# Two macaron stages on one core: cosines later in the queue of VectorE, and half of the residual added on GpSimd

## The chip, the cores and the metric

One core of a Trainium2 chip runs the whole program. The metric is the device time of one execution in microseconds (us). The time before is the median of three runs.

## The reference, cut to what matters

The program is a chain of six blocks on `x`, 16 sequences of 256 tokens with 128 channels: a macaron half block, attention with ALiBi, the same half block again, a mixture of experts, linear attention, and the mixture of experts again. The change lies in the first kind, which runs twice:

```python
x = x + 0.5 * _L0_ffn_ref(_layernorm(x), ...)     # twice, attention between them

def _layer(x, wqkv, qs, ksc, wo, lg, lb, w1, b1, w2, b2):
    q, k, v = split(shift_token(x) @ wqkv)        # 8 heads of 64
    q, k = rotary_xpos(l2norm(q) * qs, l2norm(k) * ksc)
    x = x + local_attention(q, k, v) @ wo         # windows of 64, one back
    h = layernorm(shift_token(x)) * lg + lb
    a, g = split(h @ w1 + b1)
    return x + (a * gelu(g)) @ w2 + b2

for l in range(2):                                # DEPTH
    x = _layer(x, wqkv[l], ...)
```

So the running value `y` of a sequence goes through two layers, and then `x = x + 0.5 * y`.

## The kernel before, in words

Engines are named PE (TensorE), DVE (VectorE), ACT (ScalarE), POOL (GpSimd). Each has its own queue, and the order in each queue is written out by hand; semaphores, one per kind of step, hold them together. `X` holds the residual stream of all sequences with channels on partitions, `Y` the running value of the stage, with its upper 64 channels shifted by one token, so that `shift_token` costs nothing. That is why steps on `Y` that have to undo the shift come in two halves of 64 partitions (`halves()`).

A stage `ffn(f)` works through 32 items: 16 sequences in layer 0 (items 0 to 15), then the same in layer 1 (16 to 31). It is software pipelined. In step k, counted from 0, item k is new (projections `qk`, squares, rotation, norm), item k-1 is in the middle (scores, maxima, exponentials, `attend`) and item k-2 is old (output projection, layer norm, up, gelu, `gated`, down, `resid2`). While k is 13 or less, layer norm of sequence k+2 is prepared beside it (`x_center`, `x_square`, `x_rstd`, `normed`). I speak of a step from one start of `k_out` (line 910) to the next, which is once in each k from 1 on.

What each engine does in a step, in its order:

- DVE: `o_norm(i-2, 1)`, `k_out` (L910, L911), `resid` (L975), `cosines` of tile 0 (L924), `s_max` of group 0 (two L948), `y_center` (L981), `s_max` of groups 1 and 2 (L953), `m_split`, `y_normed` (L985), `sums` of tile 0 (L930), `m_out` (L969), `cosines` and `sums` of tile 1, `clip` (L935), `gated` (three L992), `x_center` (L1013), `qk_norm` of tile 0 (L941), `resid2` (L1000 and, in layer 1, L1006), `qk_norm` of tile 1, `o_norm(i-1, 0)` (L916).
- POOL: for each of two tiles `sines` (two L490) and `rotated` (L498, the sum of cosine and sine parts, so it waits for the cosines of the tile), then `split_h` of the next item (L515, L517) and `normed` (two L505).
- ACT: copies of q and k out of PSUM (L594) and their squares (L599), `square` and `rstd` of the layer norm, `copy_v`, `gelu` with a table load ahead and behind it, `x_square` (L649), `rnorm` (L607, L608), which waits for `clip`, then three exponentials (L622), `recips` and `x_rstd`.
- PE: `qk_T` (L1332), `qk(i, 0)` (L1323 to L1325), `proj` (L1464), `scores` (L1339 and L1392), `y_mean`, `qk(i, 1)`, whose second half (g = 1) waits for `s_max` of group 0 because it writes into that PSUM bank, `y_var`, `v_proj`, `m_T`, `up`, `x_mean`, `scores_T`, `down`, `attend(i-1, 0)` (from L1445, waits for two of the exponentials), `x_var`, `attend(i-1, 1)`.

Two chains matter. `clip`, `rnorm`, the exponentials and `attend` follow one another through three engines. And `qk_norm` of a tile waits for both `rnorm` and `rotated`. The second part of `qk_T`, after which the next `k_out` starts, waits for `o_norm(i-1, 0)`.

In layer 1 `resid2` adds the down product and b2 to `Y` (L1000, two halves), waits for it, and adds half of `Y` to `X` (L1006, two halves).

## Time and profile before

| | us |
|---|---|
| median of three runs | 2471.24 (2462.63 to 2471.93) |
| the profiled execution | 2476.3 |
| its span | 2474.5 |

| engine | busy us | share of the span |
|---|---|---|
| PE | 2133.3 | 86% |
| DVE | 1762.1 | 71% |
| ACT | 1464.2 | 59% |
| POOL | 1056.6 | 43% |

The mean granted clock of TensorE is 0.94 of full speed. The two stages `ffn(0)` and `ffn(1)` lie from about 60 to 880 us and from about 1270 to 2084 us of the span.

In the timeline rows below, the first number is the start in us from the span's start, the second the duration in us, then engine, line, operation, what it writes and reads, shapes and count; in brackets stands how long the engine sat idle before it and what it waited for. Neighbours that are alike are merged into one row with their count, and the duration is then that of all. Rows of one engine can overlap by some 0.1 us, since an instruction starts while the one before is still draining.

### The profile page before, as it was taken

The numbers are of one execution on the slowest core, as the hardware profiler recorded it, in microseconds if no ns is written. First come the engines' busy times: TensorE is split into PE (matmuls) and PEld (weight loads), VectorE is DVE, ScalarE is ACT, GpSimd is POOL, SyncE is SP. The second block draws the span as 40 slices with busy tenths as digits, with TensorE's granted clock in tenths as the row PEclk, the third lists the DMA queues.
The fourth block names the chain that finished last, engine by engine and source line by source line (L and its number), as shares of the span: only waits on it lengthen the run. The fifth ranks groups of instructions, "written<-read, shape, count | busy, mean of one in ns | idle before, by whom it ended". The sixth has DMA issues, their size and how long they took to land. (4 is left out here: it accounts for less than half of the span.)

```text
span 2474.5 us, 56322 instructions
## 1 busy us (share of the span) xinstructions
PE 2133.3 (86%) x23398; PEld 1572.0 (64%) x23398; DVE 1762.1 (71%) x2815; ACT 1464.2 (59%) x2389; POOL 1056.6 (43%) x800
## 2 busy tenths in 40 slices
PE   2799999999889868999878999999999897597968
PEld 1477676666666645555536767766666664495758
DVE  3678788788788637777727787887888884563556
ACT  0577676666666525666536776766667674363635
POOL 4656555454545210000036565555545450550245
PEclk8899999999999969999959999999999998698979
DMA  7000000089999990000000000000000003121022
GB/s 150 1 2 2 2 2 2 2 88 119 113 134 133 135 133 6 2 2 2 2 1 1 2 2 2 2 1 2 2 2 2 1 1 74 56 66 37 35 75 79
DMA packets 211376, 90.91 MB, mean 37 GB/s; under 512 B 79700, under 2 KB 206721, under 8 KB 210996
## 3 DMA queue, kind: packets, MB, share of 16 engines
q1 hardware_dynamic: 202596, 72.27, 23.7%
q0 software_dynamic: 6080, 11.76, 1.5%
q10 hardware_dynamic: 2448, 3.28, 0.6%
q8 instruction: 187, 3.06, 0.6%
q14 instruction: 65, 0.53, 0.1%
HBM read 24.31 MB, written 63.41 MB: 35 GB/s over the span
## 5 line engine op out<-in xcount | busy, mean ns | idle before, releaser
L490 POOL TENSOR_TENSOR work<-work,rot_tables 128x512 f32<-128x512 f32 x256 | 411.0, 1626 | 483.8 <-ACT work L594 483.8
L498 POOL TENSOR_TENSOR work<-work 128x1024 f32<-128x1024 f32 x128 | 304.5, 2379 | 53.0 <-DVE work L924 45.7
L1323 PE MATMUL psum<-qkv_w_hi,h_hi 128*128 128x512 f32 x384 | 189.6, 494 | 90.0 <-DVE small L948 87.7
L924 DVE TENSOR_TENSOR work<-work,rot_tables 128x1024 f32<-128x1024 f32 x128 | 211.0, 1648 | 19.2 <-ACT work L594 17.4
L941 DVE TENSOR_TENSOR work<-work,small 128x1024 f32<-128x1024 f32 x128 | 166.9, 1306 | 76.3 <-ACT small L608 72.1
L1081 DVE TENSOR_REDUCE small<-psum 128x4 f32<-128x1024 f32 x128 | 156.6, 1224 | 88.3 <-PE psum L1582 86.6
L1482 PE MATMUL psum<-centered,ffn_w 128*128 128x256 f32 x768 | 192.2, 402 | 3.0 <-DVE centered L985 2.9
L705 ACT ACTIVATE work<-psum 128x1024 f32<-128x1024 f32 x128 | 131.1, 1024 | 92.7 <-PE psum L1582 92.6
L1420 PE MATMUL psum<-work 64*128 64x128 f32 (+1 forms) x2048 | 179.3, 305 | 0.0
L632 ACT ACTIVATE squared<-centered 128x256 f32<-128x256 f32 x64 | 26.8, 419 | 244.9 <-DVE centered L981 244.9
L1482 PEld LDWEIGHTS psum<-centered,ffn_w 128*128 128x128 f32 x768 | 147.7, 199 | 30.7 <-DVE centered L985 4.5
L1453 PE MATMUL psum<-work,v 128*32 128x192 f32 (+1 forms) x4096 | 163.0, 299 | 0.3 <-issue 0.3
L1323 PEld LDWEIGHTS psum<-qkv_w_hi,h_hi 128*128 128x128 f32 x384 | 74.7, 195 | 138.5 <-DVE small L948 114.2
L1325 PE MATMUL psum<-qkv_w_hi,h_lo 128*128 128x512 f32 x384 | 157.0, 409 | 2.1 <-issue 2.1
L1324 PE MATMUL psum<-qkv_w_lo,h_hi 128*128 128x512 f32 x384 | 156.4, 407 | 0.0
L930 DVE TENSOR_REDUCE small<-qk_squares 128x16 f32<-128x1024 f32 x128 | 154.9, 1210 | 1.5 <-ACT qk_squares L599 1.5
L622 ACT ACTIVATE work<-psum 128x768 f32<-128x768 f32 (+1 forms) x192 | 155.1, 873 | 0.9 <-PE psum L1420 0.8
L505 POOL TENSOR_TENSOR y_all<-centered,squared 64x256 f32<-64x256 f32 x64 | 46.8, 731 | 246.1 <-ACT squared L654 243.6
L559 POOL DMA_INDIRECT h_area<-rows,position x64 | 62.9, 983 | 198.9 <-DVE position L1163 172.3
L763 ACT ACTIVATE qk_squares<-psum,work 128x128 f32<-128x128 f32 x312 | 89.3, 369 | 91.8 <-PE psum L1742 91.8
L1420 PEld LDWEIGHTS psum<-work 64*128 64x128 f32 x2048 | 142.9, 188 | 0.0
L594 ACT ACTIVATE work<-psum 128x1024 f32<-128x1024 f32 x128 | 130.5, 1020 | 16.0 <-PE psum L1325 16.0
(279 smaller groups left out, 5401.9 us busy)
## 6 DMA issues: line engine op xcount, KB each, us to landing
h_area<-mean_weights SPq DMA_DIRECT2D x24, 2048.0 KB, 27.7
tile_x<-h_area SPq DMA_DIRECT2D x39, 128.5 KB, 2.1
stage<-in_consts ACTq DMA_DIRECT2D x1, 2817.0 KB, 12.0
tile_x<-h_area SPq DMA_DIRECT2D x39, 64.5 KB, 1.8
work<-in_x SPq DMA_DIRECT2D x4, 512.0 KB, 27.7
expert_w<-in_ew SPq DMA_DIRECT2D x1, 2048.0 KB, 8.6
expert_w<-in_ew SPq DMA_DIRECT2D x8, 256.0 KB, 6.8
work<-y_tokens SPq DMA_DIRECT2D x4, 512.0 KB, 6.2
```

Source lines behind the costliest of these rows:

```text
L490: last = pool.tensor_tensor(b[:, :, :, o_], a[:, :, :, i_], tab[:, l, 1, t, :, o_].unsqueeze(2).to_broadcast([P, 2, HEADS, 32]), ALU.mult)
L498: pool.tensor_tensor(rC[:, t, :], rC[:, t, :], rB[:, t, :], ALU.add).then_inc(f_sum, 1)
L622: act.activation(PT[:, hs, a:a + w].rearrange("p (h b) j -> p b h j", b=2), PS[:, bs, 0:m * w].rearrange("p b (h j) -> p b h j", h=m), ACT ...
L924: dve.tensor_tensor(g(rC[:, t, :]), g(rA[:, t, :]), tab[:, l, 0, t, :, :].unsqueeze(2).to_broadcast([P, 2, HEADS, DH]), ALU.mult)\
L941: dve.tensor_tensor(c_, c_, sm[0][:, 96 + 16 * t:112 + 16 * t].unsqueeze(2).to_broadcast([P, 16, DH]), ALU.mult).then_inc(f_nrm, 1)
L1081: dve.tensor_reduce(dst, PS[:, 0:2, :].rearrange("p b (t j) -> p b t j", t=TILES), AX, ALU.max, negate=True).then_inc(a_smax, 1)
L1323: pe.matmul(out, hi, w_hi, start=True, stop=False)
L1324: pe.matmul(out, hi, w_lo, start=False, stop=False)
L1325: return pe.matmul(out, lo, w_hi, start=False, stop=True)
L1420: last = pe.matmul(PS[:, bs[h % 2], o:o + w], kT[rows_(h), h // 2, j * P:(j + 1) * P], qT[rows_(h), h // 2, i0:i0 + w], start=False, stop= ...
L1453: last = pe.matmul(PS[32 * q:32 * q + 32, (4, 2)[a], z * T + lo:z * T + hi], V[i % 2][:, j, d:d + 32], PT[:, 4 * a + q, src:src + hi - lo] ...
L1482: last = pe.matmul(PS[:, b, o:o + T], fw[:, l, o2 + c * P:o2 + (c + 1) * P], ycen[:, :], start=True, stop=True)
```

## The change

It has four parts.

1. In the queue of DVE, `cosines(i, 0)` moves from ahead of `s_max(i-1, 0)` to behind `y_normed`. Behind it come `m_out`, `sums(i, 0)`, `cosines(i, 1)`, then `gated(i-2)`, which stood behind `clip` and now stands ahead of `sums(i, 1)` and `clip`.
2. In layer 1, POOL makes half of `Y` as it is after `resid` and before the down product (two scalings of 64x256 into `ocen`) and adds it to `X` (one sum of 128x256). It does so in steps k = 18 to 33, between `rotated` of tile 0 and `sines` of tile 1.
3. In layer 1, `resid2` no longer writes `Y`. One DVE instruction of 128x256 adds down product, b2 and `X` into `X`. For this the w2 and b2 of layer 1 are halved once at the start, on DVE.
4. Those who waited for `f_res2` of every item now wait for `f_res2` in layer 0 and for `x_done` in layer 1 (`items_done`).

```diff
+        def items_done(eng, i):
+            f, k = (i - 1) // ITEMS, (i - 1) % ITEMS
+            if i > 0 and k < SEQS:
+                eng.wait_ge(f_res2, f * SEQS + k + 1)
+            elif i > 0:
+                eng.wait_ge(x_done, 2 * SEQS * f + k - SEQS + 1)
...
+                def half_resid(i):
+                    _, s = layer_of(i)
+                    pool.wait_ge(f_res, i + 1)
+                    pool.wait_ge(f_sum, min(2 * (i + 2) + 1, 2 * ITEMS * (f + 1)))
+                    n = 3 * (f * SEQS + s)
+                    for h, (r, c) in enumerate(halves()):
+                        pool.tensor_scalar(ocen[r, :], Y[r, s, c], 0.5, None, ALU.mult).then_inc(f_half, 1)
+                        pool.wait_ge(f_half, n + h + 1)
+                    pool.tensor_tensor(X[:, s, :], X[:, s, :], ocen[:, :], ALU.add).then_inc(f_half, 1)
+                    pool.wait_ge(f_half, n + 3)
+
-                for k in range(-2, ITEMS):
+                for k in range(-2, ITEMS + 2):
                     i = f * ITEMS + k
                     for t in range(TILES):
-                        if k >= 0:
+                        if 0 <= k < ITEMS:
                             sines(i, t)
                             rotated(i, t)
+                        if t == 0 and k - 2 >= SEQS:
+                            half_resid(i - 2)
...
-            last.then_inc(fold, 1)
+            link(last)
+            w2r = rest[DEPTH - 1][:, o3 - o1:o3 - o1 + HC * P]
+            link(dve.tensor_scalar(w2r, w2r, 0.5, None, ALU.mult))
+            dve.tensor_scalar(b2[:, DEPTH - 1:DEPTH], b2[:, DEPTH - 1:DEPTH], 0.5, None, ALU.mult).then_inc(fold, 1)
...
+                    if l < DEPTH - 1:
                         for r, c in halves():
+                            last = dve.scalar_tensor_tensor(out=Y[r, s, c], in0=PS[r, 7, 0:T], scalar=b2[r, l:l + 1],
+                                                            in1=Y[r, s, c], op0=ALU.add, op1=ALU.add)
+                        last.then_inc(f_res2, 1)
+                    else:
+                        dve.wait_ge(f_half, 3 * (f * SEQS + s + 1))
+                        dve.scalar_tensor_tensor(out=X[:, s, :], in0=PS[:, 7, 0:T], scalar=b2[:, l:l + 1],
+                                                 in1=X[:, s, :], op0=ALU.add, op1=ALU.add).then_inc(x_done, 1)
...
-                    if new:
-                        cosines(i, 0)
                     if mid:
                         s_max(i - 1, 0)
...
                     if old:
                         y_normed(i - 2)
                     if new:
-                        sums(i, 0)
+                        cosines(i, 0)
                     if mid:
                         m_out(i - 1)
                     if new:
+                        sums(i, 0)
                         cosines(i, 1)
+                    if old:
+                        gated(i - 2)
+                    if new:
                         sums(i, 1)
                         clip(i)
-                    if old:
-                        gated(i - 2)
```

## Rows read from the trace of the kernel before

**Rows 1.** Waits of PE in the whole run: total, times, longest, in us.

```profile
PE psum L1323 <- DVE small L948: 87.7, 61, 2.0
```

**Rows 2.** Stretches of one step: length, busy PE, PEld, DVE, ACT, POOL, clock, DMA.

```profile
299.63:323.44 23.81, 22.93 (x278) 16.82 (x274) 19.03 (x28) 17.32 (x27) 14.23 (x10) 1.00 0.01 2
394.85:417.58 22.73, 21.79 (x274) 16.20 (x269) 18.40 (x27) 16.24 (x24) 13.73 (x8) 1.00 0.01 2
1631.48:1655.31 23.83, 21.79 (x274) 16.20 (x270) 19.48 (x28) 16.24 (x24) 12.74 (x8) 1.00 0.01 1
741.54:765.61 24.07, 22.02 (x274) 16.28 (x269) 20.23 (x29) 16.23 (x24) 12.73 (x8) 1.00 1.24 125
```

**Rows 3.** DVE in one step with k over 17: start, duration, line.

```profile
745.97 2.33 DVE L924 TENSOR_TENSOR work<-work,rot_tables 128x1024 f32<-128x1024 f32 x1
748.34 1.29 DVE L948 TENSOR_REDUCE small<-psum 128x4 f32<-128x512 f32 x2
...
752.15 0.43 DVE L985 TENSOR_TENSOR centered<-centered,squared 128x256 f32<-128x256 f32 x1
752.50 1.21 DVE L930 TENSOR_REDUCE small<-qk_squares 128x16 f32<-128x1024 f32 x1
...
753.96 1.51 DVE L924 TENSOR_TENSOR work<-work,rot_tables 128x1024 f32<-128x1024 f32 x1
...
756.62 0.18 DVE L935 TENSOR_SCALAR small<-small 128x32 f32<-128x32 f32 x1
756.79 1.27 DVE L992 SCALAR_TENSOR_TENSOR gated<-psum,b,gelu 128x256 f32<-128x256 f32 x3
...
760.95 0.98 DVE L1000 SCALAR_TENSOR_TENSOR y_all<-psum,b,y_all 64x256 f32<-64x256 f32 x2 [0.39 <-PE psum L1493]
761.97 0.85 DVE L1006 SCALAR_TENSOR_TENSOR x_all<-y_all,x_all 64x256 f32<-64x256 f32 x2
762.85 1.23 DVE L941 TENSOR_TENSOR work<-work,small 128x1024 f32<-128x1024 f32 x1
764.11 1.29 DVE L916 TENSOR_TENSOR o_T<-psum,work 128x512 f32<-128x512 f32 x2
```

**Rows 4.** PE in the same step.

```profile
745.65 0.73 PE L1392 MATMUL psum<-kT_bf,qT_bf 64*128 64x128 bf16 x16
...
747.31 0.40 PE L1325 MATMUL psum<-qkv_w_hi,h_lo 128*128 128x512 f32 x1
749.68 0.50 PE L1323 MATMUL psum<-qkv_w_hi,h_hi 128*128 128x512 f32 x1 [1.97 <-DVE small L948]
```

**Rows 5.** POOL in the same step.

```profile
744.72 2.50 POOL L490 TENSOR_TENSOR work<-work,rot_tables 128x512 f32<-128x512 f32 x2 [7.64 <-ACT work L594]
...
753.11 3.48 POOL L490 TENSOR_TENSOR work<-work,rot_tables 128x512 f32<-128x512 f32 x2 [2.31 <-ACT work L594]
756.67 2.36 POOL L498 TENSOR_TENSOR work<-work 128x1024 f32<-128x1024 f32 x1
```

**Rows 6.** POOL and DVE together in another step, at its clip.

```profile
679.70 2.36 POOL L498 TENSOR_TENSOR work<-work 128x1024 f32<-128x1024 f32 x1
...
679.93 2.16 DVE L935 TENSOR_SCALAR small<-small 128x32 f32<-128x32 f32 x1
```

**Rows 7.** ACT in three steps: that from 741.54, from 299.63, from 394.85.

```profile
758.72 0.23 ACT L607 ACTIVATE small<-small 128x32 f32<-128x32 f32 x1
...
315.72 0.42 ACT L649 ACTIVATE squared<-centered 128x256 f32<-128x256 f32 x1
316.04 0.21 ACT L607 ACTIVATE small<-small 128x32 f32<-128x32 f32 x1
...
410.93 0.23 ACT L607 ACTIVATE small<-small 128x32 f32<-128x32 f32 x1
```

**Rows 8.** Two POOL lines over the whole run: ns min/median/max, starts, shapes.

```profile
L515 POOL CAST h_hi<-y_all x64: 387/397/1397, 63.8 to 2011.8; 128x256 fp32r<-128x256 f32 x64
...
L505 POOL TENSOR_TENSOR y_all<-centered,squared x64: 717/732/742, 62.1 to 1608.0; 64x256 f32<-64x256 f32 x64
```

More of the change, by code:

```diff
@@ L295, in build @@
             ("st", "p", "den", "o", "rec", "o_norm", "proj", "resid")]
-        f_mean, f_cen, f_lsq, f_var, f_rstd, f_norm, f_up, f_g, f_u, f_down, f_res2 = [sem(f"ffn_{n}") for n in
-            ("mean", "centered", "squared", "var", "rstd", "normed", "up", "gelu", "gated", "down", "resid2")]
+        f_mean, f_cen, f_lsq, f_var, f_rstd, f_norm, f_up, f_g, f_u, f_down, f_res2, f_half = [sem(f"ffn_{n}") for n in
+            ("mean", "centered", "squared", "var", "rstd", "normed", "up", "gelu", "gated", "down", "resid2", "half_resid")]
         o_mean, o_cen, o_sq, o_var, o_rstd = [sem(f"pre_{n}") for n in
@@ L512, in split_h @@
                     else:
-                        pool.wait_ge(f_res2, i - SEQS + 1)
+                        items_done(pool, i - SEQS + 1)
                     free(pool, f_qk, 3 * (i - 1))
@@ L998, in resid2 @@
                     dve.wait_ge(f_down, i + 1)
-                    for r, c in halves():
-                        last = dve.scalar_tensor_tensor(out=Y[r, s, c], in0=PS[r, 7, 0:T], scalar=b2[r, l:l + 1],
-                                                        in1=Y[r, s, c], op0=ALU.add, op1=ALU.add)
-                    last.then_inc(f_res2, 1)
-                    if l == DEPTH - 1:
-                        dve.wait_ge(f_res2, i + 1)
-                        for r, c in halves():
-                            last = dve.scalar_tensor_tensor(out=X[r, s, :], in0=Y[r, s, c], scalar=0.5, in1=X[r, s, :],
-                                                            op0=ALU.mult, op1=ALU.add)
-                        last.then_inc(x_done, 1)
+                    if l < DEPTH - 1:
+                        for r, c in halves():
+                            last = dve.scalar_tensor_tensor(out=Y[r, s, c], in0=PS[r, 7, 0:T], scalar=b2[r, l:l + 1],
[5 more added lines that the diff above has]
+                                                 in1=X[:, s, :], op0=ALU.add, op1=ALU.add).then_inc(x_done, 1)
                 def x_center(n):
@@ L1460, in proj @@
                     pe.wait_ge(f_on, 2 * i + 2)
-                    free(pe, f_res2, i)
+                    items_done(pe, i)
                     pe.wait_ge(o_rstd, min(f * SEQS + i % ITEMS + 4, SEQS * (f + 1)))
@@ L1503, in x_var @@
                     pe.wait_ge(o_sq, n + 1)
-                    free(pe, f_res2, f * ITEMS + max(n % SEQS - 3, 0))
+                    items_done(pe, f * ITEMS + max(n % SEQS - 3, 0))
                     pe.matmul(PS[:, 7, T:2 * T], ones[:, :], osq[:, :], start=True, stop=True).then_inc(o_var, 1)
```

## The prediction

> **What bounds the kernel now.** I read the waits of TensorE (PE) first. In the two macaron stages `ffn(0)` and `ffn(1)` one wait stands above all others: the second group of `qk(i, 1)` waits for `s_max(i-1, 0)`, 87.7 us in 61 waits [rows 1]. The reader is to see there that the releaser is VectorE (DVE), a pair of reduces of 1.29 us together [rows 3], not long ones. The table by stretch takes four single steps, each from one start of `k_out` to the next [rows 2]: 23.81 us where a sequence is still being prepared beside it (k = 1 to 13), 22.73 (k = 14), 23.83 (k = 15 to 17) and 24.07 (k = 18 to 31). TensorE is busy 22 to 23 of these, at full clock. So these 31 steps, twice, are near TensorE's own time but for this wait.
>
> The DVE rows of one step of the last kind [rows 3] show why. Times below are from its `k_out`, at 741.54. The cosines of tile 0 stand in the queue ahead of `s_max`: they start at 4.43 and end at 6.76, and only then do the two reduces run, to 8.09. TensorE's last matmul before is at 5.77, its next could issue at about 6.02, and it issues at 8.14 [rows 4].
>
> The same rows show a second thing. The cosines take 2.33 there, 1.51 for tile 1, and L941, of the same size, 1.23. The GpSimd (POOL) rows [rows 5] give the reason: two sines ran from 744.72 to 747.22, and the cosines ended 1.08 after that. In tile 1 the cosines end at 755.47, and the second sine, 1.25 by itself, ends 1.12 later, at 756.59. So an instruction of one engine waits until that of the other is through, and goes on about 1.1 after it. The clip `L935`, 0.18 by itself, took 2.16 where the 2.36 us rotation of GpSimd had started 0.23 before it [rows 6]. `gated`, which reads PSUM, keeps its duration beside the same rotation. The Trainium skill, SBUF — State Buffer, section "SBUF: two separate sides", has this as an exclusive lock that the first comer holds for its whole instruction. These rows bear that out.
>
> **The change, part by part.** *Cosines behind `y_normed`.* `s_max` waits for its scores alone: its scores are the first eight of sixteen matmuls that take 0.73 from 4.11 [rows 4], so with the hand-over it starts at about 4.55. It ends at 5.86, and TensorE goes on at 6.02 in place of 8.14: its part of the step moves up 2.12, and `y_normed` with it, from 10.61 to 8.49. From there DVE's queue counts. With the spacings of the rows [rows 3]: cosines 0 at 8.84 to 10.07; `m_out` and `sums` 0 (1.46 from 752.50 to 753.96) from 9.97; cosines 1 ask at 11.43. GpSimd could not add up tile 0 before 10.12, and its 2.36 end at 12.48. Cosines 1 therefore end at 13.58, 1.1 later.
>
> *`gated` ahead of `sums` 1 and `clip`.* Now `clip` starts 1.15 after the end of cosines 1, `sums` 1 between them. `gated`, 1.27 of which 0.08 overlap its neighbour, comes in too: 13.58 + 1.15 + 1.19 = 15.92. ScalarE's `rnorm` waits for `clip`, and its exponentials and TensorE's `attend` wait behind `rnorm`. Before, `clip` was at 15.08 and `rnorm` at 17.18 [rows 7], behind a table load; moved up by 2.12 it could run at 15.06. Now `clip` is last.
>
> Where a sequence is prepared, `x_center` follows `clip` on DVE, and ScalarE squares it before `rnorm`. `clip` 15.92 to 16.10 (the second sine ends at 13.58 + 1.12 + 1.25 = 15.95, so it hardly waits), `x_center`, of the size of `y_normed` (0.43), 16.09 to 16.51, square 16.55, and `rnorm` 0.33 behind the square as now: 16.88. It was at 16.41 [rows 7], and the step ended 7.40 after it. So 24.28 in place of 23.81: **0.47 longer, 13 steps, +6.1.** The 1 us that TensorE gains in the front of such a step is given back.
>
> k = 14: now `rnorm` at 16.08 [rows 7] and 6.65 to the end. New: `rnorm` 16.14, but GpSimd's rotation 1 (16.03 to 18.45, behind `clip`) holds up `qk_norm` 0 to 19.55; the residual (0.95) and `qk_norm` 1, behind the split of h, end at 21.6, `o_norm` at 22.3, and k_out comes 0.81 after `o_norm` as at 764.80 [rows 3]: 23.1, +0.35. The three steps that take 23.83 now come to the same 23.1: -2.2.
>
> *Half the residual on GpSimd, k = 18 to 31.* It goes between rotation 0 and the sines of tile 1: two scalings of 64x256, one add of 128x256, each waited for. No row shows a scaling on GpSimd. The nearest are the cast of 128x256, 0.40, one input, and the product of 64x256, 0.73, two inputs [rows 8]; I take 0.45, near the one with one input, and keep 0.40 to 0.73 (nothing lets it cost less than a cast). The Trainium skill, GPSIMD Engine Reference, section "Elementwise — side-by-side cycle accounting", gives 769 ns for 512 elements at best, so an estimate of 0.38 for 256; by it the sum would be 4 us less. The add: 512 columns take 1.25 and 1024 take 2.36 [rows 5], so 256 take 0.69. A wait between them costs 0.08 (756.59 to 756.67). The first has its 0.13 of start behind it when cosines 1 let go: 0.32 + 0.08 + 0.45 + 0.08 + 0.69 + 0.08 = 1.70. So the sines start at 15.28, the first ends at 16.53, `clip` (asked 15.92) at 16.66, `rnorm` 16.70; sine 2 ends at 17.78, `qk_norm` 0 at 18.88, rotation 1 at 21.12, the cast of `split_h`, next in GpSimd's queue, at 21.52, `qk_norm` 1 at 22.62, `o_norm` at 23.28, and the next `k_out` at 24.09. It is at 24.07 now: **no gain in 14 steps.** In place of TensorE's wait stands GpSimd's queue: cosines late, rotation, half, sines, rotation in a row. Behind these waits in its queue is `split_h(i+1)`, which ends by 23.2, in time for `qk(i+1, 0)`.
>
> *The down product in one sum.* It removes the two 64x256 of L1006 (0.85) [rows 3] and makes one 128x256 of the two of L1000 (0.98): -1.35 of DVE in such a step, beside GpSimd's queue, so worth nothing there. At the stage's end, where nothing is beside it, it is worth 1.35, and the step before some 0.35: -1.7. The new wait for `f_half` (15.2) is 2 us ahead of the down product; behind it in DVE's queue would stand `qk_norm` 1. Halving w2 and b2 at the start is two small DVE instructions, 384 columns at no more than 0.46 (1.23 for 1024) and 0.18, ahead of the first mean: +0.6. The new waits `items_done` count other semaphores of the same events: nothing.
>
> **Sum.** Each stage +6.1 + 0.35 - 2.2 + 0 - 1.7 = +2.5; twice 5, and 0.6: **+5.6** on the 2476.3 of the profiled execution (span 2474.5), so 2481.9. That execution is 5.1 above the median of the runs, 2471.2. On the median: **2477**.
>
> **Rivals.** *The clip falls behind rotation 1.* In the preparation steps `clip` asks at 15.92, and rotation 1 at 15.95 + 0.08 = 16.03: 0.11 between them. If `gated` is that much later, `clip` waits out the 2.36, as in [rows 6]: `rnorm` 19.2, +2.8 in 13 steps, +2.4 for k = 14, +1.3 in three: 41 a stage in place of 2.5, **2554**. For it: the margin. Against it: the margin now is 0.05 (756.62 and 756.67), and the clip takes 0.18 there. It decides in the whole row of steps at once, since they repeat.
>
> *The half sum is dear:* 0.73 a scaling, +0.56 in 28 steps, **2492**.
>
> *GpSimd fits better:* 0.40 a scaling, and `qk_norm` 1 before the cast (-0.40): -0.5 in 28 steps, **2463**.
>
> *No engine holds the other up after all,* in the new order: `clip` near 15.0, TensorE's wait gone and nothing late in its place, so all but some 6 of the 87.7: **2389**. Against it are [rows 3], [rows 5] and [rows 6].
>
> **How the numbers follow.** Forecast 0.50, clip behind the rotation 0.14, dear half 0.13, better fit 0.18, nothing held up 0.05. The forecast alone is 2477 +- 9. The range reaches to the dear half and beyond the better fit, 2445 to 2510, and leaves out the first and the last rival, 0.19 together. A measurement can tell about 0.5%, 12.4 us, from no change. Faster by more: 0.05 + 0.10 of the better fit + 0.05 of the forecast, where I have laid something out too late, = 0.20. Slower by more: 0.14 + 0.11 of the dear half + 0.15 of the forecast's upper part = 0.40. The rest, 0.40, within.
>
> **What would show it.** TensorE's wait for L948 falls from 87.7 to under 10, which all but the clock agree on. In its place TensorE waits, at the first matmul of `attend`, for ScalarE's exponentials, over 1 us a step. Cosines of tile 0 take 1.23, those of tile 1 about 2.2, each. Clip in steps 18 to 31 stretches to some 0.7. Steps come to 24.3, 23.1 and 24.1. It is wrong if the preparation steps are shorter than 23.8 (DVE not late), near 26.6 (the clip waits out the rotation), or if steps 18 to 31 leave 23.5 to 24.7.

## The result, and the profile after

| | kernel before | changed kernel |
|---|---|---|
| median, us (runs) | 2470.86 (4) | 2505.61 (4) |
| lowest to highest, us | 2462.63 to 2471.93 | 2504.51 to 2509.64 |
| profiled execution, us | 2476.3 | 2504.51 |
| its span, us | 2474.5 | 2502.4 |

The changed kernel is slower: the ratio to the kernel before is 1.0139, with a 95% interval of 1.0109 to 1.017. That is inside the range of the prediction (2445 to 2510), but 28.6 above its figure of 2477 and 4 below its upper end; slower by more than 0.5% had a chance of 0.40. One of the ten executions of `order_only` below, 3387.78 us at a mean granted clock of 0.555, is in its median but not in its ratio.

The busy times of the changed kernel (engine, us, share of the span, instructions):

```profile
PE 2132.2 (85%) x23398; PEld 1577.1 (63%) x23398; DVE 1740.5 (70%) x2721; ACT 1463.6 (58%) x2389; POOL 1156.7 (46%) x896
```

TensorE has the same work as before (2133.3), DVE has 22 us less, GpSimd has 100 us more. TensorE's waits have other releasers (total, times, longest, us):

```profile
PE psum L1468 <- ACT work L643: 57.1, 62, 3.9
PE psum L1355 <- DVE o_T L940: 52.6, 29, 1.9
```

The wait for the maxima, 87.7 us in 61 [rows 1], has no row of more than 0.2 us now. In its place stand the wait of `attend` (L1468) for the exponentials and, 29 times, the wait of `qk_T` (L1355) for `o_norm` of up to 1.9 us.

Single steps of the changed kernel, in the columns of [rows 2]; the last two rows are the first 5 us of the two steps above them:

```profile
306.14:330.38 24.24, 22.88 (x278) 16.82 (x272) 20.11 (x29) 17.32 (x27) 14.12 (x10) 1.00 0.01 2
403.10:426.31 23.21, 21.88 (x274) 16.29 (x268) 20.30 (x27) 16.23 (x24) 12.62 (x8) 1.00 0.01 2
597.31:623.87 26.56, 23.48 (x274) 17.44 (x270) 18.82 (x27) 16.34 (x24) 15.78 (x11) 0.94 1.22 125
623.87:648.83 24.96, 21.87 (x274) 16.28 (x269) 18.82 (x27) 16.23 (x24) 15.86 (x11) 1.00 1.19 113
597.31:602.30 4.99, 4.99 (x22) 3.79 (x18) 1.92 (x2) 4.02 (x4) 1.02 (x1) 0.66 1.11 157
623.87:628.80 4.93, 4.93 (x51) 3.55 (x47) 3.13 (x5) 3.91 (x4) 1.75 (x2) 1.00 1.27 135
```

The steps with k over 17 come in two lengths, 24.96 at a granted clock of 1.00 and 26.56 at 0.94, 14 of each kind. All steps of both profiled executions, each from one start of `k_out` to the next, give this table (mean of each kind, in us, stage `ffn(0)` / stage `ffn(1)`):

| | before | after | forecast after | change in both stages |
|---|---|---|---|---|
| k = 1 | 24.83 / 24.63 | 27.18 / 25.21 | | +2.9 |
| k = 2 to 13 | 23.81 / 23.81 | 24.24 / 24.24 | 24.28 | +10.4 |
| k = 14 | 22.73 / 22.73 | 23.21 / 23.22 | 23.1 | +1.0 |
| k = 15 to 17 | 24.51 / 23.85 | 23.19 / 23.18 | 23.1 | -6.0 |
| k = 18 to 31 | 24.92 / 24.40 | 25.75 / 25.74 | 24.09 | +30.4 |

What lies outside these steps became 10.8 shorter in sum: from the last `k_out` of the first stage to the first of the second 458.42 to 452.97, behind the last of the second 429.9 to 423.8, and 0.7 more ahead of the first. The sum, 30.4 + 10.4 + 1.0 - 6.0 + 2.9 - 10.8, is the 27.9 by which the two spans differ. So most of the loss is in the 28 steps that have the half sum; the 24 preparation steps lose what was forecast for them.

DVE in the step from 623.87, of that kind:

```profile
632.71 1.22 DVE L948 TENSOR_TENSOR work<-work,rot_tables 128x1024 f32<-128x1024 f32 x1
...
635.30 2.21 DVE L948 TENSOR_TENSOR work<-work,rot_tables 128x1024 f32<-128x1024 f32 x1
...
639.86 0.18 DVE L959 TENSOR_SCALAR small<-small 128x32 f32<-128x32 f32 x1
640.69 1.70 DVE L965 TENSOR_TENSOR work<-work,small 128x1024 f32<-128x1024 f32 x1 [0.65 <-ACT small L629]
642.32 0.47 DVE L1030 SCALAR_TENSOR_TENSOR x_all<-psum,b,x_all 128x256 f32<-128x256 f32 x1
646.09 1.32 DVE L965 TENSOR_TENSOR work<-work,small 128x1024 f32<-128x1024 f32 x1 [3.31 <-POOL work L506]
647.34 1.28 DVE L940 TENSOR_TENSOR o_T<-psum,work 128x512 f32<-128x512 f32 x2
```

POOL in the same step:

```profile
634.07 2.37 POOL L506 TENSOR_TENSOR work<-work 128x1024 f32<-128x1024 f32 x1 [4.54 <-DVE work L948]
636.60 2.56 POOL L534 TENSOR_SCALAR centered<-y_all 64x256 f32<-64x256 f32 x2 [0.16 <-POOL work L506]
639.24 0.73 POOL L536 TENSOR_TENSOR x_all<-x_all,centered 128x256 f32<-128x256 f32 x1
640.04 3.49 POOL L498 TENSOR_TENSOR work<-work,rot_tables 128x512 f32<-128x512 f32 x2
643.62 2.37 POOL L506 TENSOR_TENSOR work<-work 128x1024 f32<-128x1024 f32 x1
645.94 0.40 POOL L523 CAST h_hi<-y_all 128x256 fp32r<-128x256 f32 x1
```

PE in the same step, its two waits:

```profile
642.32 0.75 PE L1468 MATMUL psum<-work,ones 128*32 128x192 f32 x16 [0.77 <-ACT work L643]
...
648.07 0.96 PE L1355 MATMUL psum<-eye,work 64*128 64x64 f32 x24 [1.89 <-DVE o_T L940]
```

The reader is to see one chain. From 634.07 to 646.34 GpSimd has no idle time over 0.16: rotation, half, sines, rotation, cast. DVE sits idle for 3.31 before its second `qk_norm` (646.09), behind rotation 1; `o_norm` comes behind it, and TensorE sits idle for 1.89 before `qk_T` can go on. The two scalings (L534) are long. The first starts with cosines 1 still at work, which end at 637.51; the pair ends at 639.16, 1.65 later, where the forecast had 0.85 for this (0.32 + 0.08 + 0.45). Over the whole run one scaling takes (ns min/median/max):

```profile
L534 POOL TENSOR_SCALAR centered<-y_all x64: 842/848/1632, 508.6 to 2104.1; 64x256 f32<-64x256 f32 x64
```

0.85 us, where the forecast had 0.45 and the range had 0.73 as its upper end.

### The profile page after: what moved, and what is told of

Same layout as the page of the kernel before. It is cut to its first block and busy times, and to the rows that moved or that the text cites. A ratio compares the mean times of both kernels' runs of the same rounds, so it can differ in the third digit from the quotient of the medians.

```text
span 2502.4 us, 56418 instructions
## 1 busy us (share of the span) xinstructions
PE 2132.2 (85%) x23398; PEld 1577.1 (63%) x23398; DVE 1740.5 (70%) x2721; ACT 1463.6 (58%) x2389; POOL 1156.7 (46%) x896
## 3 DMA queue, kind: packets, MB, share of 16 engines
q8 instruction: 187, 3.06, 0.6%
## 5 line engine op out<-in xcount | busy, mean ns | idle before, releaser
L498 POOL TENSOR_TENSOR work<-work,rot_tables 128x512 f32<-128x512 f32 x256 | 384.1, 1521 | 258.5 <-ACT work L615 256.3
L965 DVE TENSOR_TENSOR work<-work,small 128x1024 f32<-128x1024 f32 x128 | 209.2, 1636 | 146.1 <-POOL work L506 95.0
L948 DVE TENSOR_TENSOR work<-work,rot_tables 128x1024 f32<-128x1024 f32 x128 | 219.9, 1718 | 12.6 <-ACT work L615 12.6
L1505 PE MATMUL psum<-centered,ffn_w 128*128 128x256 f32 x768 | 185.8, 392 | 3.2 <-DVE centered L1009 2.9
L726 ACT ACTIVATE work<-psum 128x1024 f32<-128x1024 f32 x128 | 131.0, 1024 | 91.2 <-PE psum L1605 90.9
L635 ACT ACTIVATE work<-psum 128x1024 f32<-128x1024 f32 x64 | 65.7, 1027 | 152.7 <-PE psum L1355 152.7
L1468 PE MATMUL psum<-work,ones 128*32 128x192 f32 (+1 forms) x2048 | 96.1, 306 | 57.1 <-ACT work L643 57.1
L562 POOL CAST h_hi<-centered 128x256 fp32r<-128x256 f32 x16 | 6.4, 398 | 296.2 <-DVE centered L1087 296.2
L615 ACT ACTIVATE work<-psum 128x1024 f32<-128x1024 f32 x128 | 130.4, 1019 | 21.3 <-PE psum L1348 21.3
L999 DVE TENSOR_TENSOR y_all<-y_all,psum 64x256 f32<-64x256 f32 x128 | 53.7, 420 | 126.7 <-PE psum L1487 125.9
## 6 DMA issues: line engine op xcount, KB each, us to landing
work<-in_x SPq DMA_DIRECT2D x4, 512.0 KB, 27.9
```

The lines of the kernel that those rows point to most:

```text
L498: last = pool.tensor_tensor(b[:, :, :, o_], a[:, :, :, i_], tab[:, l, 1, t, :, o_].unsqueeze(2).to_broadcast([P, 2, HEADS, 32]), ALU.mult)
L948: dve.tensor_tensor(g(rC[:, t, :]), g(rA[:, t, :]), tab[:, l, 0, t, :, :].unsqueeze(2).to_broadcast([P, 2, HEADS, DH]), ALU.mult)\
L965: dve.tensor_tensor(c_, c_, sm[0][:, 96 + 16 * t:112 + 16 * t].unsqueeze(2).to_broadcast([P, 16, DH]), ALU.mult).then_inc(f_nrm, 1)
L1505: last = pe.matmul(PS[:, b, o:o + T], fw[:, l, o2 + c * P:o2 + (c + 1) * P], ycen[:, :], start=True, stop=True)
```

## The experiments

Each step length below is a mean of the profiled execution over the steps of that kind, in both stages; "base" is the length of most of them, at clock 1.00. Ratios are to the kernel before on the same chip, with 95% intervals.

**One part alone: the order.** `order_only` is the kernel before with the new order in DVE's queue, and the residual as it was.

```diff
                         resid(i - 2)
-                    if new:
-                        cosines(i, 0)
                     if mid:
                         s_max(i - 1, 0)
...
                     if new:
-                        sums(i, 0)
+                        cosines(i, 0)
                     if mid:
                         m_out(i - 1)
                     if new:
+                        sums(i, 0)
                         cosines(i, 1)
-                        sums(i, 1)
-                        clip(i)
                     if old:
                         gated(i - 2)
+                    if new:
+                        sums(i, 1)
+                        clip(i)
```

> The kernel before with the new DVE order alone; the half sum stays on DVE. Theory A (the half sum on GpSimd, two scalings of 0.85 us in the queue between rotation 0 and the sines, is what costs; the order alone only trades TensorE's wait for a late clip): steps 2 to 13 take 24.24, 14 to 17 take 23.2, 18 to 31 about 24.0 with few dips of TensorE's clock, 2470 to 2480 us in all. Rival B (the order alone makes steps 18 to 31 long, by the late cosines): these steps take 25 us and more, 2495 to 2510 us.

Measured: steps 24.24, 23.19, 23.20 and, for k over 17, 24.10, none of them with a lower clock, as theory A had it. Median 2466.8, ratio 1.0002 (0.9985 to 1.002). So the order alone moves nothing in sum: it loses 0.43 in each preparation step, as forecast, and gains it back in the steps with k over 14. The prediction had no forecast for the order alone; this run shows that the preparation steps are the order's doing, not the half sum's. For k over 17 the rows of a step, of DVE and then of PE, show what is late once the wait for `s_max` is gone:

```profile
755.74 0.97 DVE L1000 SCALAR_TENSOR_TENSOR y_all<-psum,b,y_all 64x256 f32<-64x256 f32 x2
756.75 0.85 DVE L1006 SCALAR_TENSOR_TENSOR x_all<-y_all,x_all 64x256 f32<-64x256 f32 x2
```

```profile
759.64 0.96 PE L1332 MATMUL psum<-eye,work 64*128 64x64 f32 x24 [1.04 <-DVE o_T L916]
```

It is DVE's queue itself: the 0.85 of the residual stand ahead of the second `qk_norm` and of `o_norm`. The steps k = 14 to 17, without L1006, take 0.9 less. Taking that instruction off DVE is thus worth 0.9 a step in the new order, if whatever replaces it costs nothing on the path.

**The other part alone: the half sum.** `half_only` is the changed kernel with the old order in DVE's queue.

```diff
                         resid(i - 2)
+                    if new:
+                        cosines(i, 0)
                     if mid:
                         s_max(i - 1, 0)
...
                     if new:
-                        cosines(i, 0)
+                        sums(i, 0)
                     if mid:
                         m_out(i - 1)
                     if new:
-                        sums(i, 0)
                         cosines(i, 1)
-                    if old:
-                        gated(i - 2)
-                    if new:
                         sums(i, 1)
                         clip(i)
+                    if old:
+                        gated(i - 2)
```

> The changed kernel with the DVE order of before: the half sum on GpSimd, the down product in one sum. Theory A: rotation 0 is done early there, the half falls into GpSimd's idle time, steps 2 to 13 stay at 23.80 and steps 18 to 31 come to some 23.8; 2458 to 2472 us. Rival C (work on GpSimd with two more readers of the shared port costs wherever it stands): steps 18 to 31 over 24.6, 2485 us or more.

Measured: base 24.14 for k over 17, but 12 of the 28 steps take 24.7 to 26.8 at a clock of 0.93 or 0.94, where the kernel before has six at such a clock. Median 2476.31, ratio 1.0046 (1.0019 to 1.0073). The gain that the first theory expected (23.80) did not come. TensorE's wait is as it was:

```profile
PE psum L1346 <- DVE small L972: 87.6, 61, 2.0
```

In this order the half sum pushes the sines of tile 1 against cosines 1, which take 1.93 in place of 1.51 [rows 3], and the clip comes 0.5 later. The base is 0.08 above that before, so most of what these steps cost beyond it is at the lower clock, with the same wait of TensorE.

Alone the two parts give 0.0% and +0.5%, together +1.4%. So the excess is an interaction. What the rows of both show is that cosines 1 late on DVE and the half sum on GpSimd stand one behind the other only where both are there.

**The suspected cost taken away.** `half_as_copy` is the changed kernel with copies for the two scalings (the factor 0.5 on this part of the residual is left out).

```diff
-                        pool.tensor_scalar(ocen[r, :], Y[r, s, c], 0.5, None, ALU.mult).then_inc(f_half, 1)
+                        pool.tensor_copy(ocen[r, :], Y[r, s, c]).then_inc(f_half, 1)
```

> The changed kernel with the two scalings by 0.5 replaced by plain copies of the same size (the factor is left out). Theory A: each takes 0.40 to 0.45 in place of 0.85, steps 18 to 31 fall from 24.95 by as much as GpSimd is relieved, to 24.1, and the steps of 26.56 go too, since TensorE's idle stretch of 1.9 us ahead of the step shrinks to about 1; 2470 to 2482 us. Rival D (the place of the three instructions counts, not their length; or the 26.56 have another cause): under 10 us gained on the changed kernel.

Measured: 23.88 for k over 17, all steps alike, median 2455.51, ratio 0.995 (0.9931 to 0.9969). The copy and TensorE's wait for `o_norm`:

```profile
L534 POOL COPY centered<-y_all x64: 389/400/1211, 507.6 to 2048.0; 64x256 f32<-64x256 f32 x64
```

```profile
PE psum L1355 <- DVE o_T L940: 12.5, 29, 0.5
```

Two instructions that are 0.45 shorter each, 0.90 together, make the base step 1.07 shorter (24.95 to 23.88), so all of their time lies on the path. And the 1.6 us that half of the steps had on top, at a lower clock, are gone with them: over the 28 steps the two profiled executions differ by 52 us, 28 x 1.07 = 30 by the base and 22 by the clock. The mechanism is theory A's; the total went below the expected 2470 to 2482, and the steps below 24.1.

This run also has nearly the price that the prediction took (0.40 for its 0.45), and with it the chain that the prediction drew. GpSimd's sines and DVE's clip in the step that starts at 1761.71:

```profile
1776.95 2.48 POOL L498 TENSOR_TENSOR work<-work,rot_tables 128x512 f32<-128x512 f32 x2
```

```profile
1777.69 0.55 DVE L959 TENSOR_SCALAR small<-small 128x32 f32<-128x32 f32 x1
```

The sines start at 15.24 of the step (15.28 was said), the clip stretches to 0.55 behind the first sine (some 0.7 was said), rotation 1 ends at 21.04 (21.12) and the step takes 23.87 (24.09).

**The same work at another place in GpSimd's queue.** `half_early` is the changed kernel with the half sum ahead of rotation 0, where GpSimd sat idle for 4.5 us. The semaphore count that it waits for is one less, since that rotation has not run yet.

```diff
-                    pool.wait_ge(f_sum, min(2 * (i + 2) + 1, 2 * ITEMS * (f + 1)))
+                    pool.wait_ge(f_sum, min(2 * (i + 2), 2 * ITEMS * (f + 1)))
...
                         if 0 <= k < ITEMS:
                             sines(i, t)
-                            rotated(i, t)
                         if t == 0 and k - 2 >= SEQS:
                             half_resid(i - 2)
+                        if 0 <= k < ITEMS:
+                            rotated(i, t)
```

> The changed kernel with the half sum ahead of rotation 0 in GpSimd's queue, where GpSimd sits idle 4.5 to 5.3 us waiting for the cosines. Theory A: the half costs nothing there, steps 18 to 31 come to about 23.1 without dips, 2440 to 2450 us, 55 less than the changed kernel. Rival C: its instructions hold up the maxima's split and y_normed on DVE instead, steps 18 to 31 at 24 or more, 2465 us or more.

Measured: 22.87 for most steps with k over 17 (means 23.05 and 22.87), all at a clock of 1.00, and those with k = 2 to 17 as in the changed kernel. Median 2437.87, ratio 0.9886 (0.9855 to 0.9917). That is theory A, a little below its numbers. POOL in one of these steps:

```profile
1849.48 1.77 POOL L534 TENSOR_SCALAR centered<-y_all 64x256 f32<-64x256 f32 x2
1851.34 0.74 POOL L536 TENSOR_TENSOR x_all<-x_all,centered 128x256 f32<-128x256 f32 x1
1854.06 2.36 POOL L506 TENSOR_TENSOR work<-work 128x1024 f32<-128x1024 f32 x1 [1.99 <-DVE work L949]
```

The scalings cost what they cost before, 0.85 each, and GpSimd still has 1.99 to spare before rotation 0. So it was never the work, but its place: some 2.5 us of GpSimd cost 2.08 a step where another engine waits behind them (24.95 against 22.87), and nothing that shows in a gap. This run also shows what taking the residual off DVE is worth once nothing hides it. These steps are 1.23 shorter than those of `order_only`, of the 1.35 that left DVE.

**That gap, overfilled.** `half_early_triple` is `half_early` with the two scalings done three times over; the counts of the semaphore `f_half` go from 3 to 7 a sequence with them.

```diff
-                    for h, (r, c) in enumerate(halves()):
+                    for h, (r, c) in enumerate(halves() + halves() + halves()):
```

> The kernel half_early with the two scalings done three times over (six of 0.85 us). GpSimd had 1.99 us of idle time left ahead of rotation 0; 3.5 us more overrun it by 1.5. Theory A: rotation 0 and everything behind it in that queue come 1.5 later, and steps 18 to 31 grow from 22.86 by 1.2 to 1.7, to 24.1 to 24.6. Rival C (each GpSimd instruction costs DVE or TensorE time of its own): they grow by 2.5 us or more.

Measured: base 24.64 (24.1 to 24.6 was expected), six of 28 steps 25.16 to 25.35 at a clock of 0.93; 2487.34 in its one run. In a step six scalings take 6.28 where two took 1.77, and rotation 0 starts 13.55 behind `k_out` where it started at 10.22, 3.33 later; the gap of 1.99 took the rest. Of these 3.33 the step got 1.77 longer, so there was still some 1.5 of slack between GpSimd's queue and TensorE. The scaling costs 0.85 here too, and TensorE waits for `o_norm` again:

```profile
L534 POOL TENSOR_SCALAR centered<-y_all x192: 839/847/1695, 502.3 to 2081.4; 64x256 f32<-64x256 f32 x192
```

```profile
PE psum L1356 <- DVE o_T L941: 40.8, 28, 1.8
```

**The square behind the exponentials.** `half_early_xsq` is `half_early` with ScalarE's `x_square` moved behind the three exponentials, so that `rnorm` waits for `clip` alone and not, in its queue, for `x_center` and its square.

```diff
-                    if pre:
-                        x_square(n)
                     if new:
                         rnorm(i)
                     if mid:
                         for q in range(3):
                             exps(i - 1, q)
+                    if pre:
+                        x_square(n)
```

> The kernel half_early with ScalarE's x_square moved from ahead of rnorm to behind the three exponentials. Theory A (what makes steps 2 to 13 0.44 longer than before is the chain clip, x_center, x_square, rnorm): rnorm no longer waits for x_center and comes 0.7 us earlier, steps 2 to 13 fall from 24.24 to 23.4 to 23.7, the other steps stay; 2420 to 2430 us. Rival E (another chain, TensorE's own time or o_norm, is level with it): steps 2 to 13 stay over 24.0, within 6 us of half_early.

Measured: 23.93 for k = 2 to 13, the others as in `half_early`. Median 2422.34, ratio 0.982 (0.9791 to 0.9848). The preparation steps lose 0.31, so the square was indeed on their path, but less than the 0.5 to 0.8 expected, and they stay 0.12 above what they took before the change. That this rest is `gated` ahead of `clip` is likely and not shown.

**`clip` ahead of `gated`.** `gated_last_early` is `half_early` with `gated` behind `clip`, as it was before the change.

```diff
-                    if old:
-                        gated(i - 2)
                     if new:
                         sums(i, 1)
                         clip(i)
+                    if old:
+                        gated(i - 2)
```

> The kernel half_early with gated back behind clip. If an engine waits for the instruction of the other on the shared port, clip now asks just when the second sine has begun and takes 1.2 to 1.4 us in place of 0.18, gated is 2.4 us later and TensorE waits for it: steps 2 to 13 near 25, steps 18 to 31 near 24.5, 2480 us or more. If the port matters little (rival), clip and with it rnorm come a good 1 us earlier and steps 2 to 13 fall under 24.0.

Measured: steps of 26.4 (k = 2 to 13), 26.0, 27.3 and 27.3, longer than expected; 2626.76 in its one run. At a clock of 1.00 the preparation steps take 25.27, near the 25 expected, but only six of the 24 have that clock. DVE and PE in a step with k over 17, and that whole kind of wait over the run:

```profile
1860.18 1.21 DVE L960 TENSOR_SCALAR small<-small 128x32 f32<-128x32 f32 x1
1861.31 1.26 DVE L1017 SCALAR_TENSOR_TENSOR gated<-psum,b,gelu 128x256 f32<-128x256 f32 x3
```

```profile
1862.62 0.54 PE L1365 MATMUL psum<-masks_bf,eye_bf 64*64 64x384 bf16 x4 [2.82 <-DVE gated L1017]
```

```profile
PE psum L1365 <- DVE gated L1017: 157.7, 60, 3.1
```

The clip asks during the second sine, and takes 1.21 in place of 0.18, as expected. `gated` stands behind it, and TensorE waits for `gated` by 2.82. What no theory had is the clock:

```profile
1818.03:1845.35 27.32, 24.52 (x274) 17.88 (x268) 20.58 (x27) 16.33 (x24) 15.01 (x11) 0.88 0.01 2
```

In every step with k over 17 the granted clock is 0.87 or 0.88, and TensorE is busy 24.5 with the same 274 matmuls that take it 21.65 in `half_early`. So `gated` ahead of `sums` 1 is worth keeping in this order of the cosines.

**Both cosines together.** `pair_early` is `half_early` with both `cosines` first, then `m_out`, both `sums`, `clip`, `gated`.

```diff
                     if new:
                         cosines(i, 0)
+                        cosines(i, 1)
                     if mid:
                         m_out(i - 1)
                     if new:
                         sums(i, 0)
-                        cosines(i, 1)
-                    if old:
-                        gated(i - 2)
-                    if new:
                         sums(i, 1)
                         clip(i)
+                    if old:
+                        gated(i - 2)
```

> The kernel half_early with both cosines in a row, then m_out, both sums, clip, gated, x_center. Cosines 1 ask 0.15 us ahead of rotation 0 and take 1.23 in place of 2.21; rotation 0 starts 1.1 later. By theory A the port's wait moves to clip, which takes some 1.1 us behind the first sine, and gated comes 1.3 later than in half_early: TensorE's wait for gated grows to 1.6 us, steps 18 to 31 take 23.3 to 23.6 in place of 22.86. Rival: the wait is gone for good and these steps keep 22.9 or less.

Measured: 23.93 for k = 2 to 13 and 23.03 for k = 14 to 31, 22.9 or less for k = 1; 2428.79 in its one run. The 23.03 lie between the two theories: the clip does wait, as theory A said, but the step grows by less than it said. Now rotation 0 waits for cosines 1, not the other way round: it is asked for between the two and takes 3.19. The two cosines take 2.35 together, nothing added. The clip takes 0.85 in place of 0.18, held up by the first sine:

```profile
1861.60 2.35 DVE L949 TENSOR_TENSOR work<-work,rot_tables 128x1024 f32<-128x1024 f32 x2
...
1866.57 0.85 DVE L960 TENSOR_SCALAR small<-small 128x32 f32<-128x32 f32 x1
```

TensorE waits for `gated` in its turn (74.3 us in 60 waits, at most 1.5), so it is no better than `half_early` for k over 17 (23.03 and 22.87), and better by 0.17 in k = 14 to 17, by 0.31 in k = 2 to 13 and by 3.7 and 2.7 in the two steps with k = 1.

**Both together.** `pair_early_xsq` is `pair_early` with `x_square` behind the exponentials; the edit is that shown above.

> The kernels pair_early and half_early_xsq in one: both cosines in a row, clip ahead of gated, the half sum ahead of rotation 0, x_square behind the exponentials. Theory A (steps 2 to 13 wait for rnorm behind x_center and x_square; without that, TensorE's own 22.9 us and the late gated bound them): steps 2 to 13 take 23.0 to 23.5, steps 14 to 31 stay at 23.03; 2400 to 2418 us. Rival E: gated, now 1.3 us later, bounds steps 2 to 13 as it is and they stay at 23.93; 2422 us or more.

Measured: 23.80 for k = 2 to 13 and 23.03 for the others. Median 2415.58 (2410.94 to 2419.79), ratio 0.98 (0.9777 to 0.9824): the lowest median of all versions here, though its interval overlaps that of `half_early_xsq`. The expected 23.0 to 23.5 in the preparation steps did not come. DVE and then POOL there:

```profile
313.82 3.27 DVE L966 TENSOR_TENSOR work<-work,small 128x1024 f32<-128x1024 f32 x1
```

```profile
313.65 2.35 POOL L506 TENSOR_TENSOR work<-work 128x1024 f32<-128x1024 f32 x1
```

`rnorm` is early now, at 312.78, but `x_center` has moved `qk_norm` 0 to 0.17 behind the start of rotation 1, so it waits that out and takes 3.27 in place of some 1.2. That this is what bounds these steps now was not taken away in a run, so it is argued and not shown. Both theories missed: one had 23.0 to 23.5, the other 23.93.

**The rival made to happen.** The prediction's first rival, at 0.14, was that the clip falls behind rotation 1. `center_first` is `half_early` with `x_center` (0.4 us) ahead of `gated`, which moves the clip by about that.

```diff
+                    if pre:
+                        x_center(n)
                     if old:
                         gated(i - 2)
                     if new:
                         sums(i, 1)
                         clip(i)
-                    if pre:
-                        x_center(n)
```

> The kernel half_early with x_center moved from behind clip to ahead of gated, which makes clip 0.33 us later in steps 1 to 13 alone. In the changed kernel clip starts there 0.10 us ahead of rotation 1. If the port goes to whoever comes first, rotation 1 now has it when clip asks: clip takes some 2.2 us in place of 0.18, rnorm comes 1.7 us later and steps 2 to 13 take 25.9 to 26.4 in place of 24.24; the other steps stay at 23.2 and 22.9. If it is not a matter of who comes first (rival), rnorm comes no later than now, since x_square is out of its way, and these steps take 24.2 or less.

Measured: 27.3 and 27.4 for k = 2 to 13, where `half_early` has 24.24, and the steps with k over 13 as there; 2512.13 in its one run. DVE, POOL and ACT in such a step:

```profile
343.27 2.16 DVE L960 TENSOR_SCALAR small<-small 128x32 f32<-128x32 f32 x1
```

```profile
343.05 2.35 POOL L506 TENSOR_TENSOR work<-work 128x1024 f32<-128x1024 f32 x1
```

```profile
345.46 0.23 ACT L629 ACTIVATE small<-small 128x32 f32<-128x32 f32 x1 [3.03 <-DVE small L960]
```

The step itself, from one `k_out` to the next, in the columns of [rows 2]:

```profile
326.96:354.27 27.31, 24.25 (x278) 17.63 (x273) 21.45 (x28) 17.42 (x27) 13.10 (x10) 0.94 0.01 1
```

The rival's mechanism is real. `rnorm` starts at 18.50 of the step, 1.65 later than in `half_early`, as expected here (1.7). The rest of the 3.06 that such a step is longer is TensorE's clock: it is 0.94 in every one of these steps, and TensorE is busy 24.25, 1.4 more than in the changed kernel. The rival had put the step near 26.6, 2.8 above the kernel before, with `rnorm` at 19.2 and no term for the clock; 27.3 came. It is near by two errors that partly offset each other.

## Why the prediction was right, and where it was not

**The bound and its removal: right.** TensorE's 87.7 us for the maxima are gone (under 10 was said). Cosines 0 take 1.22 and cosines 1 take 2.21 (1.23 and about 2.2 were said).

**The preparation steps: right.** 24.28 was said and 24.24 measured, 12 steps a stage. `order_only` has the same 24.24, so it is the order that costs there. The chain is that of the prediction. DVE and POOL in the step from 306.14:

```profile
322.12 0.18 DVE L959 TENSOR_SCALAR small<-small 128x32 f32<-128x32 f32 x1
322.21 0.41 DVE L1036 TENSOR_TENSOR centered<-x_all,psum 128x256 f32<-128x256 f32 x1
```

```profile
322.22 2.37 POOL L506 TENSOR_TENSOR work<-work 128x1024 f32<-128x1024 f32 x1
```

Clip at 15.98 of the step (15.92 was said), `rnorm` at 16.84 (16.88), and the rotation 0.10 behind the clip (0.11). The rival of 2554 was that close, and `center_first` shows its price, but the margin held (the clip's median over the run is 0.181). TensorE's wait for the exponentials is 0.91 there and 0.77 later, where over 1 us was said.

**k = 14 to 17: right.** 23.1 was said and 23.2 measured, in this kernel and in `order_only`. (In the working, rotation 1 has 2.42, from 16.03 to 18.45, where [rows 5] has 2.36; that is 0.06.) The first stage's +2.35 at k = 1 was not in the sum (0.47 was). TensorE waits 3.87 for the exponentials there, 1.90 before, and the granted clock of that step is 0.74, 0.83 before; which of the two makes the step long no run tells apart.

**The half sum: the mechanism right, the size wrong.** By the prediction's own sign it is wrong here: it said so for the case that steps 18 to 31 leave 23.5 to 24.7, and they take 24.95 and 26.55. The step that failed is this one: "two scalings of 64x256 [...] I take 0.45, near the one with one input, and keep 0.40 to 0.73". They take 0.85 each, above both ends. The nearest rows were a cast and a product of two inputs [rows 8]; a scaling has one input, and I took the number of inputs for what sets the price. The copy of the same shape takes 0.40 and the two-input sum of 128x256 takes 0.73, so the scaling is the dearest of the three: the copy reads and writes as much, so what it computes sets the price here, not how many inputs it has. With 0.85 in place of 0.45 the working of the prediction gives 24.09 + 0.80 = 24.89, and the base is 24.95. Over 28 steps that is +22.4, and `half_as_copy` takes it away again. The rival nearest to this was the dear half, 2492 at 0.13; with 0.85 in place of its 0.73 it comes to 2499. The prediction's estimate of 0.38, worked out from a best case in the Trainium skill, GPSIMD Engine Reference, section "Elementwise — side-by-side cycle accounting", is less than half of the 0.85 that the trace has, and the trace decides.

A detail went the other way than said, by the same error. The clip was to stretch to 0.7 behind the first sine. It took 0.18, since the sines came 0.9 later than said (16.17 of the step for 15.28), and the clip got in 0.18 ahead of them. `qk_norm` 0 also got in between the two sines, which therefore take 3.49.

**The clock: not foreseen.** Of the 28 steps with the half sum 14 take 1.6 more than the base, at a granted clock of 0.94. The rows above show where: in the first 5 us of the step from 597.31 it is 0.66, and TensorE issues 22 matmuls there against 51 in the step after. Two matmuls of the same line in the two steps:

```profile
597.80 0.63 PE L1347 MATMUL psum<-qkv_w_lo,h_hi 128*128 128x512 f32 x1
...
624.34 0.40 PE L1347 MATMUL psum<-qkv_w_lo,h_hi 128*128 128x512 f32 x1
```

Before both TensorE had sat idle for about 1.90, waiting for `o_norm`. That is 22 us in the changed kernel. The kernel before had some too, 17 us above its base in these 28 steps, nearly all in six steps at a clock of 0.93 or 0.94, with its wait of 1.97 for the maxima [rows 4]; the net is +5.5. The prediction counted the granted clock as 1.00 in these steps [rows 2] and never asked what a wait does to it.

**The down product in one sum, and the tail: the term can't be told.** 1.7 less for each stage's end was said. The stretch between the stages is 452.97, but it is 452.52 in `order_only`, which has the old residual, and 456.95 in `pair_early`, which has the new one. The stretches outside the macaron stages vary by several us from kernel to kernel. So the -10.8 outside the steps, start included, in place of -2.8, is not shown to be the change's. The 0.7 at the start agrees with the 0.6 that was said, and `order_only`, which halves no weights, has 0.0.

**In sum.** +5.6 was said and +28.2 measured between the profiled executions, 22.6 more: +24.9 from the base of the 28 steps (0.89 each, nothing said), +5.5 from the clock, +1.1 from k = 1 to 13, +0.3 from k = 14, -1.6 from k = 15 to 17, where one step before was long (25.87 at a clock of 0.93), and -8.0 outside them, which adds up to 22.2; another 0.3 lies outside the two spans. The medians differ by 6.5 more, since the profiled execution of the kernel before was 5.4 above its median and that of the changed kernel 1.1 below.

That the result lies inside the range is in part luck. Within the steps it came out 30 us above the forecast; the -8.0 outside them, which no run ties to the change, brought it back under the upper end of 2510, with 4 us left.

**What stays open.** Why half of these steps get the lower clock and not all of them, and why at the same wait of 1.97 the kernel before has six such steps of 28 and `half_only` twelve. No run here tells that apart. The preparation steps are no exception to it: in the kernel before TensorE's wait for the maxima is shorter there, 0.87, and they keep 1.00 [rows 2].

```profile
306.68 0.50 PE L1323 MATMUL psum<-qkv_w_hi,h_hi 128*128 128x512 f32 x1 [0.87 <-DVE small L948]
```

Where they get a wait of 2.74, in `center_first`, all 24 have the lower clock. Nor is it settled what makes the stretches outside the steps vary.

## What to carry to other kernels

Work that goes to an idle engine is free only in that engine's gaps, not in its idle sum: here the same half sum costs 2.1 us a step or nothing that shows, by standing 7 us later or earlier in the same queue. Price an instruction on GpSimd by a row of its own operation, and let the bounds reach past the nearest rows where none is there; if the step hangs on it, put the work where a wrong price does no harm. And where VectorE and GpSimd alternate with margins of 0.1 us, look at who comes first before moving anything, since 0.4 us of a small instruction cost 3.1 us a step here, 1.4 of them by the clock.

## What the runs showed of the hardware

- A scaling (TENSOR_SCALAR, times a constant, f32, 64x256) takes 0.85 us on GpSimd, a copy of the same shape 0.40, a sum of two inputs of 128x256 0.73.
- Steps of 23 to 27 us in which TensorE has a longer wait for another engine have a lower granted clock more often. With k over 17, by the longest such wait: none of 28 steps at 0.77 (`half_early`), 1.04 (`order_only`), 1.15 (`half_as_copy`) and 1.5 (`pair_early`); six of 28 at 1.8 (`half_early_triple`); 14 of 28 at 1.9 (the changed kernel); six of 28 (the kernel before) and 12 of 28 (`half_only`) at 1.97; all 28 at 2.8 (`gated_last_early`). For k = 2 to 13: 18 of 24 at 2.36 (`gated_last_early`), all 24 at 2.74 (`center_first`), and none in any other kernel, where it is 1.1 or less. So between 1.8 and 2.4 the wait alone does not decide. Where the clock falls in the changed kernel, matmuls of 0.40 take 0.63 for some 5 us, with a mean of 0.66 of 2.4 GHz, so it is at its lower level, 1.2 GHz, for about two thirds of that.
- DVE and GpSimd hold each other up by whole instructions, in both directions, and a margin of 0.05 to 0.2 us decides who waits: a clip of 0.18 takes 2.16 where it asks 0.22 behind a rotation, and 0.18 where it asks 0.10 ahead of one. The Trainium skill, SBUF — State Buffer, section "SBUF: two separate sides", has this as an exclusive lock between these two engines, which whoever starts first holds for its whole instruction, and these rows agree.
